# The slot of the row maxima in two small attentions: written by GpSimd instead of VectorE

## The reference

```python
q = apply_axial_rope(q, pos_map)
k = apply_axial_rope(k, ctx_pos_map)
scale = 1.0 / np.sqrt(HEAD_DIM).astype(np.float32)
logits = jnp.einsum('bqhd,bkhd->bhqk', q, k) * scale
w = jax.nn.softmax(logits, axis=-1)
attn = jnp.einsum('bhqk,bkhd->bqhd', w, v)
```

```python
scores = jnp.einsum('bqgsd,bkgd->bgsqk', q, k) * scale
causal = jnp.arange(n)[:, None] < jnp.arange(n)[None, :]
scores = jnp.where(causal, -jnp.inf, scores)
attn = jax.nn.softmax(scores, axis=-1)
```

## Time and profile before

| | before |
|---|---|
| median of 3 runs | 3481.63 us |
| lowest and highest | 3477.75, 3481.8 us |
| profiled execution | 3481.1 us |
| its span | 3479.1 us |
| mean granted clock of TensorE | 0.929 |
| PE, DVE, ACT, POOL busy | 84%, 61%, 51%, 40% of the span |

### The profile page before, as it was taken

The page is one execution under the profiler, slowest core; times in us unless marked ns, Lnnn a source line. Parts: engine busy times, 40 slices in busy tenths (PEclk is TensorE's granted clock), DMA queues, the critical chain, the costliest instruction groups (busy, mean ns, idle before and its releaser), DMA issues. The chain is left out here.

```text
span 3479.1 us, 64422 instructions
## 1 busy us (share of the span) xinstructions
PE 2910.5 (84%) x24866; PEld 2050.9 (59%) x24866; DVE 2108.0 (61%) x4574; ACT 1764.8 (51%) x3865; POOL 1404.9 (40%) x1537
## 2 busy tenths in 40 slices
PE   4989889894888886699999978887999999975777
PEld 2566555552566664577777756665766666752333
DVE  4666666665677774555555446665555555555887
ACT  3444444443788886433333246664444444454775
POOL 1333343332587886244444424442122222213453
PEclk9988998987899997799999999998999999997898
DMA  4000000001000000300000001102011110022000
GB/s 159 1 1 1 1 1 1 1 1 64 1 2 2 2 2 20 135 1 13 1 1 1 1 34 38 32 2 67 2 37 37 37 37 1 1 73 67 12 19 25
DMA packets 41189, 81.49 MB, mean 23 GB/s; under 512 B 5683, under 2 KB 9781, under 8 KB 40758
## 3 DMA queue, kind: packets, MB, share of 16 engines
q1 hardware_dynamic: 40886, 77.38, 6.5%
HBM read 73.18 MB, written 4.19 MB: 22 GB/s over the span
## 5 line engine op out<-in xcount | busy, mean ns | idle before, releaser
L960 POOL TENSOR_TENSOR c_pT<-c_prob,c_pT 128x512 f16<-128x512 f32 x256 | 293.4, 1159 | 106.4 <-ACT c_pT L917 105.7
L1813 POOL TENSOR_TENSOR c_prob<-c_prob,c_inv 128x512 f32<-128x512 f32 x128 | 133.5, 1043 | 310.6 <-DVE c_inv L2037 310.6
L960 POOL TENSOR_TENSOR a_pT<-a_prob,a_pT 128x384 f16<-128x384 f32 x128 | 120.6, 945 | 189.5 <-ACT a_pT L917 189.1
L1151 ACT ACTIVATE c_prob<-psT 128x512 f32<-128x512 f32 x256 | 155.8, 609 | 70.0 <-PE psT L1082 56.0
L1232 DVE TENSOR_REDUCE c_peak<-psS 128x2 f32<-128x512 f32 x256 | 169.8, 683 | 20.7 <-PE psS L1063 17.4
L917 ACT CAST c_pT<-c_prob 128x512 f16<-128x512 f32 x256 | 159.7, 624 | 0.0
L421 POOL TENSOR_TENSOR a_q_rot<-a_q_cos,a_q_sin 128x512 f32<-128x512 f32 x64 | 81.0, 1265 | 192.0 <-DVE a_q_sin L666 192.0
L429 POOL TENSOR_TENSOR a_prob<-a_prob,a_inv 128x128 f32<-128x128 f32 x128 | 51.1, 399 | 256.7 <-DVE a_inv L698 256.7
L596 ACT ACTIVATE a_pT<-psT,a_kvh_t 128x256 f16<-128x256 f32 (+1 forms) x256 | 93.6, 416 | 105.0 <-PE psT L442 105.0
L1961 ACT CAST c_pT<-psT 128x512 f16<-128x512 f32 x128 | 74.8, 584 | 140.0 <-PE psT L1825 140.0
L1953 ACT ACTIVATE c_prob<-psS,c_negmax 128x256 f32<-128x256 f32 x256 | 119.2, 474 | 44.8 <-DVE c_negmax L2030 41.2
(11 more groups left out here) (580 smaller groups left out, 11456.7 us busy)
## 6 DMA issues: line engine op xcount, KB each, us to landing
c_feed<-in_L_ffn_w1T SPq DMA_DIRECT2D x16, 512.0 KB, 3.6
c_feed<-in_L_ffn_w2T SPq DMA_DIRECT2D x16, 512.0 KB, 3.6
f_stage<-in_f_up_gateT SPq DMA_DIRECT2D x16, 352.0 KB, 8.0
x_all<-in_x SPq DMA_DIRECT2D x1, 4096.0 KB, 14.1
a_stage<-in_L_attn_WqT SPq DMA_DIRECT2D x8, 512.0 KB, 7.6
a_stage<-in_L_attn_WoutT SPq DMA_DIRECT2D x8, 512.0 KB, 10.0
a_feed<-in_L_xattn_Wq SPq DMA_DIRECT2D x8, 512.0 KB, 3.7
c_feed<-in_L_xattn_Wo SPq DMA_DIRECT2D x8, 512.0 KB, 3.9
```

The costliest lines, as they stand in the source:

```text
L960: pool.tensor_tensor(pT[1][:, c % NPH, :], prob[:, c % NPX, :], pT[0][:, c % NPH, :], ALU.subtract)\
L1151: act.activation(prob[:, c % NPX, :], ST[c % 2][:, 0:EW], ACT.Exp).then_inc(s.e_done, 1)
L1813: pool.tensor_tensor(prob[:, h % NPB, :, :], prob[:, h % NPB, :, :], inv[:, h % NPB, :].rearrange("p (n a) -> p n a", a=1).broadcast_to([P ...
```

## The change

GpSimd writes the slot. Its `fill_slots` stands behind `low_p(t-2)` and ahead of everything else of the step; it waits for `m_done` (the last reduction of the group) in c0 and for a new semaphore `peak_joined` in a1. On DVE the write is gone; in a1 the join of the second and third piece stays (`join_peaks`) and raises `peak_joined`, with no wait behind it. The wait for its operands ahead of the fill is gone from DVE in c0. The lines of `Scope.__exit__` only concern errors while the program is built.

```diff
+        s.peak_joined = sc.sem("peak_joined")
...
             @block.gpsimd
...
+                def fill_slots(b, g):
+                    heads = slice(g * GH, (g + 1) * GH)
+                    if causal:
+                        pool.wait_ge(s.peak_joined, NG * b + g + 1)
+                    else:
+                        pool.wait_ge(s.m_done, b * H + (g + 1) * GH)
+                    pool.tensor_scalar(q_stack[:, b % 2, :, heads, 3, 0], peak[:, heads, 0:NT].rearrange("p h n -> p n h"),
+                                       -1.0 / SHIFT, None, ALU.mult).then_inc(s.slot_done, 1)
...
                 for t in range(FIRST, LAST):
                     if 0 <= t - 2 < B * H:
                         low_p(t - 2)
+                    if (found := peak_head(t)) is not None and found[1] % GH == GH - 1:
+                        fill_slots(found[0], found[1] // GH)
                     if from_ctx:
...
             @block.vector
...
-                def fill_slots(b, g):
+                def join_peaks(b, g):
                     heads = slice(g * GH, (g + 1) * GH)
                     dve.wait_ge(s.m_done, b * H + (g + 1) * GH)
-                    if causal:
-                        step(dve.tensor_tensor(peak[:, heads, 1], peak[:, heads, 1], peak[:, heads, 2], ALU.max))
-                    dve.tensor_scalar(q_stack[:, b % 2, :, heads, 3, 0], peak[:, heads, 0:NT].rearrange("p h n -> p n h"),
-                                      -1.0 / SHIFT, None, ALU.mult).then_inc(s.slot_done, 1)
+                    dve.tensor_tensor(peak[:, heads, 1], peak[:, heads, 1], peak[:, heads, 2], ALU.max)\
+                        .then_inc(s.peak_joined, 1)
...
                         rowmax(b, h)
-                        if h % GH == GH - 1:
-                            fill_slots(b, h // GH)
+                        if h % GH == GH - 1 and causal:
+                            join_peaks(b, h // GH)
```

More of the change, by code:

```diff
@@ L90, in __exit__ @@
     def __exit__(self, *a):
+        if a[0]:
+            return False
         with self.nc.Block() as block:
```

## The result

The changed kernel takes 3492.36 us (median of 6 runs, 3489.53 to 3495.01), the kernel before 3479.19 us on the same chip (6 runs, 3472.82 to 3481.80). The ratio is 1.0041, with a 95% interval of 1.0029 to 1.0054: slower, by 13 us. The profiled executions have spans of 3490.4 and 3479.1 us, 11.3 us apart. The runs of the kernel before lie anywhere from 3472 to 3482 us, and its profiled execution (3481.1) is one of the long ones, so that a difference of two profiles can miss one of medians by some 5 us.

What follows compares the result with a forecast made beforehand. No engine alone bounds c0; only the chain from engine to engine counts. c0 +18.3, a1 -7.2 - 0.8 + 0.8, sum +11.1 us, forecast 3492.5; own range 3487 to 3498, 8 in 10 within 3479 to 3503.

Steps and rivals of the forecast that it cites:

- The wait in c0: c0, third group's fill: GpSimd waits for DVE's reduction, delaying queued work; 2.92 us six times plus 0.8, sum +18.3 us.
- It is not given back: c0: ACT has no slack and PE needs its copies, so the whole delay of 18.3 us is carried.
- The first two rivals: c0's delay is given back: at least 15 us, 3474 to 3478, chance 0.12; or 9 us, 3483.7, chance 0.13.
- DVE's relief: c0: DVE gets back 32 x 0.8 us, costed at nothing because ACT is behind DVE there.
- The price of the fill: The fill's tensor_scalar on GpSimd takes 0.25 us, with 0.13 and 0.61 as the ends.
- the third rival: The fill is dear on GpSimd, 0.61 us: 11 us more, 3503; chance 0.12.
- The other groups: c0, steps 25, 1 and 17: the fill costs 0.25 us of GpSimd, costed at nothing; without cover 6 us.
- exactly once per sequence: a1 before the change: DVE's fill is long once in each sequence, 1209 ns at most.
- The gain in a1: a1, step 5: without the fill ahead of the reciprocal, PE's wait for output rows shrinks; 7.2 us gained.
- 1.10 us earlier, and PE and ACT with it: a1, step 5: the reciprocal starts where the fill did; 6 x 1.10 + 0.6 = 7.2 us gained.
- The fourth rival: a1 gives nothing because PE's wait is followed by another: 3500 us; chance 0.08.

Runs made afterwards that it cites:

- The half-way kernel: Against the changed kernel, the fill in c0 moves behind the addition of the rotated q, still ahead of stacking and bias: 3484.98 us, ratio 1.0025.

## Why the prediction was right, and where it was not

**The wait in c0: right.** GpSimd stands 3.75 us ahead of the fill, with the four operations behind it that were named. Exponential by exponential, the delay against the kernel before jumps at that place in sequences 1 to 6, by 3.0 to 3.1 us each, and by 0.9 in the last; in the first it doesn't. That is 19.3 us where 18.3 were forecast. Most of the difference is a term that I had set to zero: the forecast took the end of the low part for the start of the exponential, and up to 0.10 us lie between. The stretch from L946's start to the low part's end was 4.79 us for 4.78. The other 2 us of the +21.5 are the rest of larger amounts. In the first sequence the exponentials come 2.6 us earlier than before, ahead of any blocked place; so they do, by 2.6 to 3.0 us, in every kernel whose c0 has the fill on GpSimd, and not in the two others that leave c0 as it was. Between the blocked places sequences 1 to 6 lose another 5.6 us, and the last one gives 0.6 back. The ups and downs in this are TensorE's clock at the heads 23 to 26 of a sequence, which take 5.4 us where it is 1.00 throughout, 6.7 to 7.0 at a mean of 0.75 and 7.7 at 0.55. Windows of these heads in sequences 3 and 4, before and after:

```profile
1123.60:1129.10 5.50, 4.06 (x69) 2.99 (x65) 4.23 (x7) 3.73 (x8) 3.76 (x4) 1.00 0.02 3
1183.70:1191.40 7.70, 6.25 (x61) 3.76 (x58) 4.78 (x9) 3.92 (x8) 3.73 (x5) 0.56 0.01 2
...
1132.60:1139.30 6.70, 5.25 (x66) 3.38 (x63) 4.20 (x7) 3.64 (x7) 3.72 (x4) 0.75 0.01 2
1197.40:1204.20 6.80, 5.35 (x68) 3.43 (x64) 4.29 (x7) 3.69 (x8) 3.77 (x4) 0.75 0.01 2
```

Over the six sequences these heads cancel (-0.3 us). Most of the remaining 1 us a sequence is ACT waiting longer for PE's scores ahead of heads 18 and 24: 0.92 us for 0.38 and 1.66 for 1.24 in sequences 2 and 5. With the fill at the end of the step the wait ahead of head 18 is 0.38 again, so it belongs to the order, too; by which way it comes about isn't shown.

**It is not given back: right.** The first two rivals ask for 9 to 15 us returned within c0. The half-way kernel gives the slope: 1.2 us less behind the wait is 1.2 us less at each place. DVE's relief of 24.6 us in c0 was costed at nothing. No run separates it from the rest of the move; it may be what the 2.6 us of the first sequence come from, and more than that it didn't buy.

**The price of the fill: right in kind.** 0.32 us in c0 and 0.26 in a1 for the 0.25 taken; the third rival's 0.61 is out. From the fill's start to the next start on GpSimd only 0.21 us pass. That the 1.03 us on DVE in c0 were mostly waiting is seen in the kernel before: 27 of its 32 fills there take more than 0.21 us, and 22 of the 27 end 0.05 to 0.07 us behind the end of an instruction of GpSimd (the other five lie beside the first of a row of two, which by the length of one would end just as close); on GpSimd all 32 take 0.31 to 0.32 us. This agrees with what the Trainium skill ("SBUF — State Buffer", "Who interferes with whom") says of the shared port pair, that whoever comes second waits for the other's whole instruction. In a1 the reading "exactly once per sequence" was not right: the fill is long (1.21 us) once in each of six sequences, never in the first, and twice (0.86 and 0.85 us) in the last. The forecast doesn't hang on this. The other groups cost nothing that shows: the second group's fill makes the exponential behind it wait up to 1.14 us for 0.85, and the next one makes that up, as forecast, and with the fill at the end of the step all of them still run and c0 is 482.9 us against 483.0.

**The gain in a1: right in sign, each place too small, and a part given back.** The step that was too small is "1.10 us earlier, and PE and ACT with it": it sums to 7.2 us, and at the seven places the exponentials come earlier by 14.9 in all (0.9 in the last sequence, 1.8 to 3.0 in the others). Two things are in that. PE's wait shrinks by 1.27 us rather than 1.10; its total goes from 17.2 to 8.6 us, 8.6 for the 7.2 of the forecast. And behind the shorter wait PE runs at the lower clock in 2 of 7 places where it did in 6; what it does there is done in less time. The gain goes with it: 2.3 to 3.0 us in the four places that are no longer at the lower clock, 1.9 and 1.8 in the two that still are, and 0.85 in the last, where it was 1.00 before and the wait is 0.85 us shorter. The prediction shifted all that stands behind PE's wait by 1.10 us and didn't ask how fast PE is there. Against this, PE waits longer for the fill, 10.3 to 12.3 us, where 0.8 was forecast (of which the exponentials show 0.12 a sequence), and 4.5 us are lost again in the first steps of the sequences, 3.0 of them in sequences 3 and 4. There the lower clock has come in where it wasn't before. Windows at these two places, after and then before:

```profile
2196.00:2198.00 2.00, 2.00 (x21) 1.97 (x19) 1.99 (x3) 1.12 (x3) 2.00 (x4) 0.50 0.80 250
2240.50:2242.50 2.00, 2.00 (x13) 1.47 (x12) 0.73 (x4) 0.31 (x2) 1.12 (x2) 0.50 0.23 77
...
2178.00:2180.00 2.00, 1.90 (x34) 1.76 (x29) 1.74 (x4) 1.98 (x5) 1.85 (x3) 1.00 0.71 253
2224.00:2226.00 2.00, 2.00 (x30) 1.85 (x29) 1.59 (x7) 1.42 (x5) 0.00 (x0) 1.00 0.16 56
```

PE's waits just ahead are a little longer than before, 1.48 and 0.93 us for 1.35 and 0.69 in sequence 3, 2.49 for 2.38 in sequence 4. The kernel with the fill on GpSimd in a1 alone has the lower clock at the same two places and repeats the pattern to 0.3 us, so it isn't chance; whether the longer waits bring it about isn't shown. Left are 9.0 us, for a forecast of 7.2. The fourth rival, no gain, is out.

**The sum.** +11.1 was forecast; the profiles differ by 11.3, the medians by 13.2. The near hit in the profiles flatters the working: c0 was 3 us over its term, and a1 gained 2 us more than its own; 1.2 us between and around the layers made up for the rest. That two misses of 2 to 3 us cancel is luck.

## What to carry to other kernels

An instruction that moves to another engine brings its wait with it, and everything queued behind it there is late until that wait ends. Look for what stands behind, piece by piece, and put the instruction where its operand is already there: that turned +13 us into -10 us with the same instructions. Judge it by when the later work starts, not by the sum of one kind of wait. And where PE stands still, read how long its next instructions take as well as how long it waits.

## What the runs showed of the hardware that I had not expected

- TensorE was at its lower clock behind 6 of 7 waits in a1 before (six of 2.54, the seventh of 1.88 us) and behind 7 of 7 with three reductions added (2.64), behind 1.73 us in 4 of 7, behind 1.27 and behind 1.06 us in 2 of 7 (the seventh wait of each is 0.24 us shorter). In most places it was at 1.00 up to the wait's end, in some it fell within the wait (0.63 and then 0.50 in the last 1.6 us of the one before 2196.11), in others only behind the transposes. A transpose that takes 0.27 us at the full clock took 0.42. With the added reductions a place newly at the lower clock cost 1.0 us beyond the wait.
- The same tensor_scalar of 16 columns took 0.20 us at best and 1.03 in the median on DVE, where 22 of the 27 long ones ended 0.05 to 0.07 us behind the end of an instruction of GpSimd, and 0.31 to 0.32 on GpSimd in every one of 32 cases.
- GpSimd starts its next instruction 0.21 us after the start of a fill that is recorded with 0.31 us.
